# Seven narrow jobs of the first half's tokens ahead of the wait for the dispatch, 25 wide and 21 narrow jobs, 18 result tiles, three shared tiles last

## The reference

```python
logits = jnp.einsum('btd,ed->bte', x, w_router)
probs = jax.nn.softmax(logits, axis=-1)
vals, idx = jax.lax.top_k(probs, TOP_K)                       # TOP_K = 2
gates = jnp.sum(jax.nn.one_hot(idx, N_EXPERTS, dtype=x.dtype) * vals[..., None], axis=-2)
hs = jax.nn.gelu(jnp.einsum('btd,fd->btf', x, Ws1) + bs1)     # the shared expert, 128 -> 512 -> 128
acc = jnp.einsum('btf,df->btd', hs, Ws2) + bs2
h = jax.nn.gelu(jnp.einsum('btd,efd->btef', x, W1) + b1)      # the 8 experts, 128 -> 512 -> 128
y = jnp.einsum('btef,edf->bted', h, W2) + b2
acc = acc + jnp.einsum('bted,bte->btd', y, gates)
```

## Time and profile before

| | |
|---|---|
| median of the timed runs | 533.71 us |
| the profiled execution, time | 532.91 us |
| its span, first to last instruction | 531.1 us |
| job list starts on TensorE | 348.4 us |
| last matmul ends | 519.0 us |
| granted TensorE clock, mean | 0.971 |

### The profile page before, as it was taken

How to read it: one execution, slowest core, us unless ns; L and a number is a source line. 1 busy time by engine, 2 the same in 40 slices (tenths; PEclk the granted TensorE clock), 3 DMA queues, 4 the chain that set the end, 5 groups by cost and what they waited for, 6 DMA issues and landing times.

```text
span 531.1 us, 13354 instructions
## 1 busy us (share of the span) xinstructions
PE 486.6 (92%) x4030; PEld 442.3 (83%) x4030; DVE 390.8 (74%) x1613; ACT 365.6 (69%) x1383; POOL 349.4 (66%) x521
## 2 busy tenths in 40 slices
PE   3699999999999999999899979899989999899790
PEld 2489999999999999999747769789979998899680
DVE  4688888888898888988678887427885663343864
ACT  3369999899999999999759588554444544555450
POOL 4257767676776767775320788888888888776640
PEclk9579999999999999999998999999999999999997
DMA  9999900000000000000000114545447788698876
GB/s 194 332 397 393 354 3 1 2 1 3 2 2 2 2 2 2 2 2 2 1 2 0 43 42 134 182 120 172 129 134 217 244 269 260 215 286 265 329 231 184
DMA packets 39277, 68.50 MB, mean 129 GB/s; under 512 B 7475, under 2 KB 25781, under 8 KB 39205
## 3 DMA queue, kind: packets, MB, share of 16 engines
q1 hardware_dynamic: 31764, 56.69, 33.4%
q0 software_dynamic: 4320, 8.99, 4.8%
q10 hardware_dynamic: 3120, 1.97, 1.3%
HBM read 38.16 MB, written 29.46 MB: 127 GB/s over the span
## 4 chain that ended last, share of the span: by engine, by line
PE 62%; POOL 16%; issue 6%; DVE 6%; DMA 5%; ACT 3%; SPq 2%; another core or an unknown queue 1%; POOLq 0%; ACTq 0%; DVEq 0%
PE bank L1418 35%; POOL xs L1287 12%; PE bank L671 8%; PE bank L685 8%; POOL rested L1276 4%; DMA xr<-in_L_attn_x_dram 1%; PE bank L653 1%; DMA xt<-xs 1%; ACT hid L805 1%; DMA yg<-ys 1%; PE bank L566 1%; SPq L217 1%; PE bank L1627 1%; PE bank L1504 1%
## 5 line engine op out<-in xcount | busy, mean ns | idle before, releaser
L1295 POOL DMA_INDIRECT ys<-yo,dst x71 | 71.6, 1008 | 30.9 <-issue 15.2
L1287 POOL DMA_INDIRECT xs<-hrow,slot_i x64 | 62.9, 984 | 38.0 <-issue 38.0
L805 ACT ACTIVATE hid<-bank,slab 128x256 f32<-128x256 f32 (+1 forms) x172 | 62.6, 443 | 29.9 <-PE bank L671 23.0
L685 PE MATMUL bank<-slab,hid 128*128 128x128 f32 x568 | 71.9, 276 | 2.9 <-issue 1.6
L685 PEld LDWEIGHTS bank<-slab,hid 128*128 128x128 f32 x568 | 69.5, 192 | 5.4 <-issue 1.8
L671 PE MATMUL bank<-hg,slab 128*128 128x256 f32 (+1 forms) x344 | 68.8, 343 | 0.5 <-ACT hg L813 0.5
L671 PEld LDWEIGHTS bank<-hg,slab 128*128 128x128 f32 x344 | 55.0, 191 | 5.2 <-issue 0.7
L1174 DVE TENSOR_TENSOR yb<-bank,slab 128x256 f32<-128x256 f32 (+1 forms) x43 | 16.2, 378 | 56.2 <-PE bank L685 32.8
L813 ACT COPY hg<-bank 128x256 f32<-128x256 f32 (+1 forms) x43 | 14.4, 338 | 49.6 <-PE bank L653 34.4
L1276 POOL MEMSET rested<- 128x1408 f32 x32 | 41.3, 1290 | 0.0
L2311 POOL TENSOR_TENSOR nH<-aH,ones 128x128 f32<-128x128 f32 x32 | 14.9, 466 | 33.8 <-ACT aH L1767 33.8
(11 more groups left out here) (423 smaller groups left out, 1809.3 us busy)
## 6 DMA issues: line engine op xcount, KB each, us to landing
slab<-in_slabs_dram SPq DMA_DIRECT2D x43, 578.0 KB
xs<-fill SPq DMA_DIRECT2D x34, 528.0 KB, 7.6
xt<-xs SPq DMA_DIRECT2D x28, 132.0 KB
yg<-ys SPq DMA_DIRECT2D x7, 512.0 KB, 5.8
out_dram<-xr SPq DMA_DIRECT2D x18, 64.0 KB
ys<-yo,dst POOLq DMA_INDIRECT x71
xr<-in_L_attn_x_dram SPq DMA_DIRECT2D x4, 256.0 KB, 6.6
xs<-hrow,slot_i POOLq DMA_INDIRECT x64
```

The source lines that it names most:

```text
L685: mm = pe.matmul(y[:, s * D:(s + 1) * D], hid[i % 2][:, n, s * P:(s + 1) * P], right, start=(n == 0), stop=(n == FT - 1), skip_group_check ...
L805: nc.scalar.activation(hid[i % 2][:, n, 0:w], e_half(i, n)[:, 0:w], ACT.Gelu_apprx_tanh, bias=bias).then_inc(e_x, 1)
L1287: pool.indirect_dma_start(out=xs[:, :], out_offset=bass.IndirectOffsetOnAxis(ap=slot_i[:, i, c:c + 1], axis=0), in_=hrow[:, c, :], in_offs ...
L1295: pool.indirect_dma_start(out=ys[:, :], out_offset=bass.IndirectOffsetOnAxis(ap=dst[v][:, s:s + 1], axis=0), in_=yo[v][:, s, :], in_offset ...
```

## The change

The job order is another one, and with it the number of tiles: 9 wide and 7 narrow tiles from rows of the first half (`N_EARLY` = 16) and two shared tiles stand ahead of the wait for `s_half[1]`, where 9 wide and five shared stood. Over all there are 25 wide and 21 narrow tiles instead of 28 and 15: 71 units of 128 rows in both. Three shared tiles end the list instead of two.

```diff
-ORDER = "WW.WW.WW.WW.W." + "WWWW" + 6 * "WH" + 2 * "WWH" + "WWWWW" + "HHHHHHH" + ".."
+ORDER = "WW.WWWWHWHWHWHH.HH" + "WWW" + 4 * "WH" + "." + 4 * "WH" + "WWWWW" + "." + "HHHHHH" + "..."
-LOAD_AT = BY_HALF + 6
 RX = 4
-RY = 10
-RW = 5
+BIASED, BIAS_AT = EARLY_SH + 2, 19
+RY = 18
...
+        hs = hid
...
             sp.wait_ge(s_half[0], 16 * CH)
-            for j in range(N_FULL):
+            for j in range(N_EARLY):
+                if j == EARLY_HALF:
+                    sp.wait_ge(table_ready, 4)
                 rows(j)
                 if j >= RW:
                     weights(j)
-            sp.wait_ge(table_ready, 4)
-            weights(N_FULL)
-            weights(N_FULL + 1)
+            sp.wait_ge(table_ready, 6)
+            weights(N_EARLY)
+            weights(N_EARLY + 1)
             sp.wait_ge(s_half[1], 16 * CH)
-            for j in range(N_FULL, N_TILES):
+            for j in range(N_EARLY, N_TILES):
                 rows(j)
...
-                if j == LOAD_AT:
-                    scattered(sp, BY_HALF)
-                if LOAD_AT <= j < LOAD_AT + 4:
-                    load(sp, j - LOAD_AT)
+            scattered(sp, BY_HALF)
+            for g in range(4):
+                load(sp, g)
             scattered(sp, BY_THREE)
             load(sp, 4)
             load(sp, 5)
...
+            def early_halves():
+                seen = past[:, 0:N, :]
+                then(dve.tensor_reduce(full_by[:, :], over[:, :, :], AX_X, ALU.add))
+                then(dve.tensor_scalar(begun[:, :], marks[:, 0:E], float(SUB), None, ALU.mult))
...
+                dve.wait_ge(table_ready, 3)
+                dve.tensor_copy(row_i[:, early], rowf[:, early]).then_inc(table_ready, 1)
+
+            def begin_rest():
+                then(dve.tensor_scalar(last[:, 0, :], last[:, 0, :], float(N), None, ALU.min))
...
-            SUMS = {-12: (0, 1), -11: (2, 3), -10: (4, 5), -9: (6,), -8: (7,), -7: (8,), -6: (9,), -5: (10,), -4: (11,), -3: (12, 13, 14, 15), -2: (16,)}
+            SUMS = {-5: (0,), -4: (1, 2, 3, 4, 5), -3: (6, 7, 8, 9, 10, 11), -2: (12, 13, 14, 15, 16, 17)}
...
                 e_post(i)
-                if i == 2:
+                if i == 0:
+                    early_halves()
+                elif i == 1:
+                    begin_rest()
+                elif i == 3:
                     rest_marks()
-                elif i == 3:
+                elif i == 4:
                     ends(marks)
```

More of the change, by code:

```diff
@@ L34 @@
 N_SH = B * S // SH
+RW = 5
 PARTS = ((0, 2), (2, 4), (4, 6), (6, 8))
@@ L419, in program @@
         first, rowf = psb("first", [P, N_TILES]), psb("rowf", [P, N_TILES])
-        hs = [psb(f"hs{i}", [P, FT, SH]) for i in range(2)]
         ysh = [psb(f"ysh{i}", [P, SUB, D]) for i in range(2)]
@@ new lines, in begin_rest @@
+            def begin_rest():
+                then(dve.tensor_scalar(last[:, 0, :], last[:, 0, :], float(N), None, ALU.min))
+                then(dve.tensor_tensor(begun[:, 1:E], begun[:, 1:E], last[:, 0, 1:E], ALU.add))
+                then(dve.tensor_tensor(begun[:, 1:E], begun[:, 1:E], last[:, 0, 0:E - 1], ALU.subtract))
+                then(dve.tensor_tensor(begun[:, 0:1], begun[:, 0:1], last[:, 0, 0:1], ALU.add))
+                then(dve.tensor_scalar(marks[:, 0:E], begun[:, :], 1.0 / SUB, None, ALU.mult))
+                then(dve.scalar_tensor_tensor(out=left[:, :, :], in0=begun[:, :].unsqueeze(1).broadcast_to([P, 3, E]), scalar=-float(P),
+                                              in1=held[:, :, :], op0=ALU.mult, op1=ALU.add))
@@ L1071, in rest_marks @@
                 dve.wait_ge(turned, NG)
-                then(dve.tensor_tensor(over_all, held[:, :, :].rearrange("p k e -> p (k e)").unsqueeze(2).broadcast_to(grid),
+                then(dve.tensor_tensor(over_all, left[:, :, :].rearrange("p k e -> p (k e)").unsqueeze(2).broadcast_to(grid),
                                        cut["step"].unsqueeze(1).broadcast_to(grid), ALU.is_gt))
@@ L1078, in rest_marks @@
                                        odd[:, 2 * E:3 * E].unsqueeze(1).broadcast_to([P, 3, E]), ALU.min))
+                then(dve.tensor_tensor(each(marks[:, E:4 * E]), each(marks[:, E:4 * E]),
+                                       marks[:, 0:E].unsqueeze(1).broadcast_to([P, 3, E]), ALU.add))
+                then(dve.tensor_tensor(each(units[:, :]), each(units[:, :]), begun[:, :].unsqueeze(1).broadcast_to([P, 3, E]), ALU.add))
             def ends(at):
@@ L1167, in e_post @@
                     dve.wait_ge(e_yb, i + 1)
-                    if j >= EARLY_SH + 5:
+                    if j >= BIASED:
                         dve.wait_ge(xs_ready, NG)
```

76 lines of the change are left out of this document (49 added, 27 removed).

## The result

The changed kernel took 540.55 us (median of 20 runs, 534.88 to 544.28) where the kernel before, beside it on the same chip, took 535.80 (20 runs, 532.38 to 543.09). The ratio is 1.0071 (95% interval 1.0040 to 1.0102): 0.7% slower, 3.8 us, where 525.4 was forecast (the two medians are 4.75 us apart). Every ratio here leaves out runs that lie over 1.5% above the fastest of the same kernel. The profiled executions stand further apart, 538.7 us of span for 531.1.

A forecast was written before the change was run, and what follows sets the result against it. TensorE, busy 92%, was taken as the bound, losing 12.2 us to stalls. 532.9 + 0.1 - 1.8 - 5.9 - 4.5 + 2.5 + 1.3 = 524.6 us profiled, 525.4 as median; 8-in-10 range 520.5 to 532.

The forecast's parts named there:

- RY from 10 to 18: Pairs, mostly 436 to 465 us: 18 result tiles end VectorE's waits in `meta(j)` for GpSimd's scatters, -5.9 us.
- The wait for the dispatch: At the second half's rows: more early jobs bring TensorE there at 400.3, after rows land at 396.5, -1.8 us.
- the stall of +1.3 in its place: First late tile's rows, behind a slab awaiting job 13's late post, land at 402.6; TensorE asks at 401.3.
- +2.5: New loss from VectorE's added early work: late posts plus late first rows at the boundary; bounds 0 and 6 us.
- Costed at nothing: Early stretch: three more slabs and seven tiles more early raise the DMA share to about 0.75, priced at zero.
- The four loads behind the last slab: From 487 to 509 us: the last narrow tiles' rows no longer stand behind `yg` loads, -4.5 us.
- The end: Behind TensorE's end: the span ends 13.4 us later where it was 12.1, +1.3 us.
- T: End of the last narrow down: 498.1 us without stall, 500.6 with it; span ends at T + 22.2.
- VectorE in the early stretch: Ahead of job 18: added tables and posts make 48 us of work in 50.8, delaying posts, +2.5 us together.
- The rule weighed: GpSimd and VectorE contend for SBUF: added operations could slow GpSimd's dispatches, giving 531.3; by the row it stays 525.4.
- a slower GpSimd: Rival in GpSimd's dispatches and scatters: long operations delay everything behind, 540 us at a mean of 1.2; chance 0.07.

The follow-up runs named there:

- groups 2 and 4: Follow-up runs of changed or repeated kernels, each group on a chip of its own; kernel before took 531.08 us (group 2) and 530.12 us (group 4).
- groups 1, 3 and 5: Follow-up runs of changed or repeated kernels, each group on a chip of its own; kernel before took 538.11, 536.19 and 538.43 us.
- with rows ahead: Changed kernel, SyncE issuing a tile's rows before the previous tile's weights: whole list 0.9931, 0.9983; from first late tile on 0.9976, 1.0108.
- without early narrow tiles: Kernel before with other edits, among them ring 18 and loads last 1.0007, these plus rows ahead behind the dispatch wait 0.9997, that order alone 0.9992.
- loads alone: Kernel before with only the four `yg` loads moved behind the last slab and their sums to the last three jobs: 0.9980.
- rows ahead over the whole list: Kernel before with each tile's rows issued ahead of the previous tile's weights throughout SyncE's loop: 1.0131.
- ring alone: Kernel before with 18 result tiles instead of 10, `hs` on the buffers of `hid`, nothing else: 1.0027.
- the early order mended: Changed kernel with rows one tile ahead of weights among the sixteen early tiles only, boundary order as changed: 1.0061.
- by halves: Changed kernel with rows ahead among the early tiles only 1.0061, or from the first late tile on only 0.9976; changed kernel beside them 1.0037.
- With the boundary mended: Changed kernel with rows one tile ahead of weights from the first late tile on: 1.0108 in group 5.
- The constant slabs: Changed kernel with slabs loaded from constant expert addresses, no register load ahead of each, output of other experts' weights: 1.0046.
- part slabs: Changed kernel loading only a slab's up weights, 512 of 1156 columns, after the first five slabs: 1.0047.

## Why the prediction was wrong

**The chips are of two kinds, and the profile of before was of one.** On the chips of groups 2 and 4 (before: 531.1 and 530.1 us) none of the eight profiles has a piece of 0.69 to 0.75 us of SyncE or of "issue" in its chains of waits from 360 to 505 us, and none has a wait for "remote" there. On the chips of the result and of groups 1, 3 and 5 (before: 535.8 to 538.4) all twelve profiles have waits for "remote", of ScalarE and of VectorE, nine have such pieces (1 to 44; the result's own has one, the kernel before's none), and the median time between two issues of SyncE, worked out from its timeline, is some 1.5 to 1.6 us for 1.2 to 1.4 in the first eight. SyncE's waits between 360 and 500 us are 47.5 us in the changed kernel of group 4 and 22.7 and 20.1 in its other two profiles. So one can't compare ratios across groups without saying the kind; within a group one can. No two of the five groups share a chip, so whether the kind is the chip's or the time's isn't shown.

| | short steps (groups 2, 4) | long steps (result, groups 1, 3, 5) |
|---|---|---|
| changed | 1.0037 | 1.0071, 1.0144 |
| with rows ahead, over the whole list or from the boundary on | 0.9931, 0.9976, 0.9983 | 1.0108 |
| without early narrow tiles | 0.9980 (loads alone), 1.0131 (rows ahead over the whole list) | 1.0007, 0.9997, 0.9992, 1.0027 (ring alone) |

Step by step:

- **"RY from 10 to 18": -5.9.** Wrong in its cause, and the largest miss. I read "remote" beside `meta(j)` as its wait for a scatter. The ring of 18 alone leaves 22.1, 13.7 and 11.6 us of "remote" and gives 1.0027; the kernel before with a ring of 10 has none on a short-step chip. It is a pause of the engines on that kind of chip. That ScalarE, which has no such wait in the program, paused with VectorE could have been read in the profile of before, where both resume within 0.03 us of each other:

```profile
463.41 0.37 ACT L813 COPY hg<-bank 128x256 f32<-128x256 f32 x1 [2.97 <-remote]
463.44 0.42 DVE L1174 TENSOR_TENSOR yb<-bank,slab 128x256 f32<-128x256 f32 x1 [3.77 <-remote]
...
479.25 0.37 ACT L813 COPY hg<-bank 128x256 f32<-128x256 f32 x1 [2.53 <-remote]
479.27 0.29 DVE L1174 TENSOR_TENSOR yb<-bank,slab 128x128 f32<-128x128 f32 x1 [3.76 <-remote]
```

The size was wrong too: 5.9 was a remainder, 12.2 less two waits that I had read, while TensorE's timeline of the kernel before shows 2.9 us of waits in all between 405 and 494 us. Every profile has 1 us or more of "over" that is no wait (3.3 in the kernel before). Measured value of the term: 0 (1.0027, interval 0.9994 to 1.0061).
- **"The wait for the dispatch": -1.8, and the stall of +1.3 in its place** (post, slab, rows: part of the +2.5). The mechanism was right to the line: the first late rows stand behind the slab that waits for tile 12's post. Its size was not: I had 4.0 us from post to landed rows, the clean chain has 5.7 (403.91 to 409.63), since a transfer of 3.78 us, not 2.00, lies in it; in the first profile of the changed kernel the slab of tile 17 also came only 2.2 us behind that of tile 16. TensorE's wait is 3.7 to 4.4 us in the four profiles of the changed kernel or of it with the early order mended, and the next feeds, ups and downs, at a lower granted clock behind it, take 1.5 to 2.7 more. Mending this order is worth 0.6% on the short-step chip, shown by halves. And the -1.8 was a matter of the start of the list: the dispatch ends on GpSimd's time, so the old wait is 3.9 us where the list starts at 347.2, 1.8 at 349.5, 0.5 at 351.6 and none at 353.4 or later, in the kernels with the old order there. At the median of the starts above, 353.4, there was nothing to take.
- **"Costed at nothing": SyncE.** I priced three more slabs as bytes (a share of 0.75) and not as instructions. In the early stretch a narrow tile lasts 1.9 us on TensorE; on a long-step chip SyncE needs 3.4 us to issue a tile's rows and slab. With the boundary mended the early tiles still cost 1.1% in the same group, with waits of TensorE of 0.4 to 1.5 us spread over 379 to 420 us, 6.1 in all. That SyncE's instructions are the limit there is read from that chain and its lack of waits, and holds for that profile; that they carry the rest of the loss on the other long-step chips is not shown. The constant slabs speak against it as the whole cause: SyncE had 47.1 us of waits there, and the ratio was 1.0046. Nor is the share of the bytes settled: over half a slab less gave 1.0047. The share of the DMA engines was 0.66 from 353 to 408 us, under the 0.75 that I had.
- **"The four loads behind the last slab": -4.5, and "The end": +1.3.** These held. In the changed kernel TensorE has no wait behind 494 us (0 and 1.9 us in the other two profiles of it) for 4.5 in the kernel before and 6.0 in its second profile; the span ends at T + 21.8 for T + 22.2 forecast, the tail is 13.1 to 13.4 for 13.4. The loads alone, without the third shared tile last, pay 3.7 us in the tail instead (16.0) and come to 0.998.
- **"VectorE in the early stretch": +1 of the +2.5.** The place was right, a post held up behind tables, and it is part of the wait at the boundary, as the chain of the fourth group shows (a post 3.3 us late for the 3.7 that I had). Over the whole stretch the sum was too high: VectorE was busy 39.9 us of 55.2 from 353 to 408 us for 48 of 50.8, though over 90% in the last 16 us in three of four profiles. Doing the added tables ahead of the list changed nothing (1.0138 beside 1.0144); the late narrow tiles' tables were not tried. There were waits at tiles 8 to 12 (1.9 us in the changed kernel's first profile, 0.7 on the short-step chip).
- **The rule weighed** in the prediction left a slower GpSimd possible. The trace decides against that here: 983 ns beside VectorE's added work, for 1008. GpSimd's last scatter ended at 519.7 and not near 503, but because TensorE was late, not it.

So from the first up on, of a forecast 12.4 - 1.8 - 5.9 - 4.5 + 2.5 = 2.7 us over the ideal time, the changed kernel shows 14.8, 20.7 and 7.4 us. The steps that failed are the ring's 5.9 us, which nothing gave back, the boundary, which lost some 6 us (4.4 of wait, 1.7 behind it at a lower clock) where it was to gain 1.8 and lose 1.3, and the early tiles' price on SyncE, put at nothing. What remains open: why some chips have the steps of 0.70 us and the pauses; it is not the amount of slab bytes, since the kernel with part slabs has them as well (10 such pieces, three lines of "remote").

A version that beats both is there on the short-step chips only: the changed kernel with rows one tile ahead (0.9931 and 0.9983 over the whole list, 0.9976 from the boundary on; under 1 beyond its interval in the first alone). On a long-step chip it is slower than the kernel before, and the kernels without early narrow tiles equal it.

## What to carry to other kernels

SyncE had a rate in instructions here as well as one in bytes: before jobs are made shorter, or moved to where they follow each other faster, count what the issuing engine does for each and look in the chain at what one takes. A wait that ends on another engine's schedule should be priced over several executions, not one; here it was 0 to 3.9 us with the start of the list. Two engines that resume at the same instant, time after time, speak for a cause that is neither's own wait in the program: an edit to the ring that one of them waits for removed nothing here. And what is left of a sum after the waits that were read is not yet a wait: add up the timeline before an edit is to win it back.

Moving a load ahead in a queue moves whatever it waits for ahead too: the same edit was worth -0.5% (beside the changed kernel, group 4) where the wait for the dispatch was already met and +1.3% where 19.8 us of it stood ahead of a slab.

## What the runs showed of the hardware

The same program differed by chip in more than its clock: SyncE's instructions came in steps of 0.69 to 0.75 us on the chips of three groups (in eight of their ten profiles) and on those of two never, with ScalarE and VectorE pausing up to 5.2 us ("remote") on the former and in the result's profiles, and the kernel before took 0.9 to 1.6% longer there. With the granted clock between 260 and 320 us, and with the kind of chip, the start of the job list moved by up to 9.5 us between profiles of programs that are alike up to there (347.2 to 356.7); on the short-step chips alone, 6 us from a clock of 0.96 to 0.88 and 0.78.
